# The last layer's K and V projections: in each group's step, or for all 16 groups at the fused stage's beginning

## The reference, cut to what matters

```python
qn = _layer_norm(x, ln1_g, ln1_b)               # x: output of layer 0
kn = vn = _layer_norm(ctx_1024, ln1_g, ln1_b)   # the context, the same for K and V
Q, K, V = qn @ wq + bq, kn @ wk + bk, vn @ wv + bv
attn = softmax(Q K^T / sqrt(8)) per head         # 16 heads of 8, not causal
x = x + (attn V) @ wo + bo
return x + gelu(_layer_norm(x) @ w1 + b1) @ w2 + b2
```

## Time and profile before

| | |
|---|---|
| median of 3 executions | 1389.48 us (1388.59 to 1390.74) |
| span of the profiled execution, first to last instruction | 1387.9 us |
| its own time as a whole | not given apart from the span; the median is 1.6 us above the span |
| mean granted clock of PE | 0.960 |
| busy over the span: PE, PEld, DVE, ACT, POOL | 89%, 75%, 68%, 71%, 65% |
| traffic | 113.96 MB, 82 GB/s in the mean |
| 900 to 1000 us (barrier, beginning of the fused stage): PE, DVE, ACT, POOL busy | 53, 55, 47, 66 of 100 us, PE clock 0.73 |
| 1000 to 1100 us (groups in full flow) | 89, 92, 88, 79 of 100 us, PE clock 1.00 |

### The profile page before, as it was taken

The page is one execution under the profiler, slowest core; times in us unless marked ns, Lnnn a source line. Parts: engine busy times, 40 slices in busy tenths (PEclk is TensorE's granted clock), DMA queues, the critical chain, the costliest instruction groups (busy, mean ns, idle before and its releaser), DMA issues. The chain is left out here.

```text
span 1387.9 us, 59975 instructions
## 1 busy us (share of the span) xinstructions
PE 1238.4 (89%) x23094; PEld 1036.4 (75%) x23094; DVE 944.3 (68%) x2136; ACT 980.7 (71%) x1956; POOL 897.7 (65%) x1432
## 2 busy tenths in 40 slices
PE   4999999989999998958999999925889998898997
PEld 2778888777788887937999999924677776675775
DVE  3788888877887886595555555525999999864331
ACT  1677787777888887346788776614888888875553
POOL 2577777777777665216999998758677777413431
PEclk9999999999999999579999999966999999999999
DMA  4233434332222320151322222322232333112221
GB/s 126 71 111 110 121 107 127 108 94 87 84 83 83 91 69 26 35 156 39 89 84 81 81 84 66 65 73 69 76 88 82 89 89 91 59 47 61 69 68 46
DMA packets 140285, 113.96 MB, mean 82 GB/s; under 512 B 17184, under 2 KB 113952, under 8 KB 140192
## 3 DMA queue, kind: packets, MB, share of 16 engines
q1 hardware_dynamic: 131744, 95.42, 23.5%
q0 software_dynamic: 8448, 17.32, 5.0%
HBM read 78.55 MB, written 34.08 MB: 81 GB/s over the span
## 5 line engine op out<-in xcount | busy, mean ns | idle before, releaser
L912 DVE TENSOR_REDUCE at_mx<-at_ps_s 128x16 f32<-128x1024 f32 x128 | 156.1, 1220 | 90.4 <-PE at_ps_s L599 46.3
L818 ACT ACTIVATE at_pt<-at_ps_t 128x1024 f32<-128x1024 f32 x128 | 130.6, 1020 | 54.7 <-PE at_ps_t L613 54.0
L811 ACT ACTIVATE at_pr<-at_dd 128x1024 f32<-128x1024 f32 x128 | 135.2, 1056 | 34.6 <-DVE at_dd L920 34.5
L2452 DVE COPY ex_wt<-experts 128x1156 f32 x133 | 102.8, 773 | 82.3 <-DVE ex_y L2458 74.0
L2410 ACT ACTIVATE ex_hg<-ex_ps_h,ex_wt 128x128 f32<-128x128 f32 x544 | 155.1, 375 | 1.2 <-PE ex_ps_y L2369 1.2
L2338 POOL DMA_INDIRECT ex_xg<-x,ex_ti x136 | 139.0, 1022 | 23.4 <-issue 21.8
L920 DVE TENSOR_TENSOR at_dd<-at_ps_s,at_mx 128x1024 f32<-128x1024 f32 x128 | 153.7, 1202 | 0.1
L2360 PE MATMUL ex_ps_h<-ex_xt,ex_wt 128*128 128x128 f32 x1088 | 147.1, 278 | 1.0 <-ACT ex_xt L2402 0.8
L1992 POOL DMA_INDIRECT l_yg<-rows,l_sl x128 | 126.1, 985 | 31.9 <-issue 29.5
L613 PE MATMUL at_ps_t<-ident,at_pr 128*128 128x128 f32 x1024 | 139.3, 279 | 6.1 <-issue 4.2
L2369 PE MATMUL ex_ps_y<-ex_wt,ex_hg 128*128 128x128 f32 x1088 | 143.7, 275 | 0.4 <-ACT ex_hg L2410 0.4
(11 more groups left out here) (262 smaller groups left out, 3154.5 us busy)
## 6 DMA issues: line engine op xcount, KB each, us to landing
rows<-ex_y SPq DMA_DIRECT2D x136, 64.0 KB
x<-at_ln_out SPq DMA_DIRECT2D x32, 256.0 KB, 3.2
at_kx<-in_xt SPq DMA_DIRECT2D x16, 256.0 KB, 2.8
at_qx<-in_xt SPq DMA_DIRECT2D x16, 256.0 KB, 2.8
at_vin<-in_xt SPq DMA_DIRECT2D x16, 256.0 KB, 2.9
at_xr<-in_x SPq DMA_DIRECT2D x16, 256.0 KB, 3.0
cx<-in_ctx SPq DMA_DIRECT2D x16, 256.0 KB, 3.2
x1t<-at_xt SPq DMA_DIRECT2D x16, 256.0 KB, 3.3
```

Source lines behind the costliest of these rows:

```text
L811: act.activation(pr[:, p], dd[:, p], ACT.Exp, scale=SCALE).then_inc(p_ready, 1)
L818: act.activation(pt[:, 2 * h + p], ps_t[:, :, :, :], ACT.Copy).then_inc(pt_ready, 1)
L912: dve.tensor_reduce(mx[:, p], ps_s[:, :, 4 * p:4 * p + 4, :], AX.X, ALU.max).then_inc(mx_ready, 1)
```

## The change

At the beginning of the fused stage PE projects K and V of all 16 groups, one after the other, out of the on-chip tile `x2t` (now called `zt` in this stage and kept alive to the end), in place of the 22 matmuls. K of group g goes into bank g % 2 of the score banks and ACT copies it back over `zt`; V goes into bank 2 + g % 2 and DVE copies it into one of 16 places in tiles that are not yet in use (`pt`, `dd`, `pr`), from where SP stores it to a memory tensor `ctxv`. These copies and stores are written into steps -3, -2 and -1 of the engines. In the steps proper `project_k` and `project_v` are gone: `mask_k` reads `zt`, and `copy_v` reads `vin`, which SP now loads from `ctxv`. The loads of `kx` and the stores of the transposed context in the two earlier stages are gone, with their waits. `hid` and `y` of the MLP now lie in `dd`.

```diff
 # sync engine, fused stage
-                    if a.shift(2).exists():
-                        load_k(a.shift(2))
+                def store_v(g):
+                    sp.wait_ge(vt_ready, g + 1)
+                    sp.dma_start(layer.kv_src[:, bass.ts(g, GT)], staged(g)).then_inc(v_out, 16)
+                    if a.unrolled and -3 <= a.g < 0:
+                        for g in ((0, 1, 2, 3, 4), (5, 6, 7, 8, 9, 10), (11, 12, 13, 14, 15))[a.g + 3]:
+                            store_v(g)
                     if a.shift(1).exists():
                         load_v(a.shift(1))            # the first waits for v_out, 16 * NG
 # tensor engine
-                spare = ps_s[:, 3].rearrange("p a b -> p (a b)")
-                pe.wait_ge(fmv_ready, 2)
-                for k in range(22):
-                    pe.matmul(spare[:, 0:P], c.ident[:, :], c.num[:, 0:P], start=True, stop=True)
+                for g in range(NG):
+                    project_k(g)                      # waits for kt_ready, g - 1
+                    project_v(g)                      # waits for vt_ready, g - 1
...
+                    else:                             # scores of the first half
+                        pe.wait_ge(kt_ready, NG)
+                        pe.wait_ge(vt_ready, NG)
...
-                        if a.shift(-1).exists():
-                            pe.wait_ge(vx_ready, g)
+                        if a.exists():
+                            pe.wait_ge(qb_ready, g + 1)
                         project_out(a.shift(-2))
...
-                    if a.shift(1).exists():
-                        pe.wait_ge(qb_ready, g + 2)
-                        project_k(a.shift(1))
...
-                    if a.exists():
-                        if a.shift(1).exists():
-                            pe.wait_ge(kb_ready, g + 2)
-                        else:
-                            pe.wait_ge(y_ready, g - 1)
-                        project_v(a)
 # scalar engine
+                def keep_k(g):
+                    act.wait_ge(early_k, g + 1)
+                    act.wait_ge(early_v, g + 1)
+                    act.activation(zt[:, bass.ts(g, GT)], bank[g % 2][:, :], ACT.Copy).then_inc(kt_ready, 1)
...
+                    if a.unrolled and -2 <= g < 0:    # first in the step
+                        for e in ((0, 1, 2, 3, 4, 5, 6, 7), (8, 9, 10, 11, 12, 13, 14, 15))[g + 2]:
+                            keep_k(e)
...
-                        ins = act.activation(kb[:, j, :], ps_g[:, :], ACT.Identity,
+                        ins = act.activation(kb[:, j, :], zt[:, bass.ts(a.place, GT)], ACT.Identity,
...
-                        src = ps_g[half, :].rearrange("p (w a m) -> p w a m", a=2, m=8)
+                        src = vin[half, :].rearrange("p (w a m) -> p w a m", a=2, m=8)
 # vector engine
+                def keep_v(g):
+                    dve.wait_ge(early_v, g + 1)
+                    dve.tensor_copy(staged(g), bank[2 + g % 2][:, :]).then_inc(vt_ready, 1)
...
+                    if a.unrolled and -3 <= g < -1:   # first in the step
+                        for e in ((0, 1, 2, 3, 4), (9, 10))[g + 3]:
+                            keep_v(e)
...
+                    if a.unrolled and -3 <= g < -1:   # after front_moments
+                        for e in ((5, 6, 7, 8), (11, 12, 13, 14, 15))[g + 3]:
+                            keep_v(e)
+                    if a.unrolled and g == -1:
+                        dve.wait_ge(v_out, 16 * NG)
                     if a.shift(1).exists():
                         maximum(g * 2 + 2, 0)
 # earlier stages
-                for g in range(NCT):
-                    sp.wait_ge(cxt_ready, g + 1)
-                    sp.dma_start(ct_out[:, bass.ts(g, GT)], layers[-1].out_tr[:, bass.ts(g, GT)]).then_inc(ct_stored, 16)
...
-                pool.wait_ge(r.ct_stored, 16 * NCT)
...
-                    if s == TU - 1 and turning:
-                        sp.dma_start(ct_out[:, bass.ts(q + NCT, GT)], xt_ctx[:, bass.ts(q + NCT, GT)]).then_inc(zc_stored, 16)
...
-                sp.wait_ge(zc_stored, 16 * (NG - NCT))
```

More of the change, by code:

```diff
@@ L1166, with __init__ @@
 class FinalStage:
-    def __init__(self, c, n, ps_s, ps_t, x_src, stored, scores_read, turned_read, w1_dram, b1_dram, w2_dram, b2, out_tok):
+    def __init__(self, c, n, ps_s, ps_t, x_src, stored, scores_read, turned_read, late, w1_dram, b1_dram, w2_dram, b2, out_tok):
         w1 = n.sb("w1", [P, FF])
@@ L1481, in fused_phase, with staged @@
         xb_ready, y_ready = n.sem("xb_ready"), n.sem("y_ready")
+        zt = layer.out_tr
+        bank = [ps_s[:, i].rearrange("p a b -> p (a b)") for i in range(4)]
+        def staged(g):
+            whole = (pt.rearrange("p h b r q -> p (h b r q)") if g < NG // 2 else
+                     dd.rearrange("p u r b s -> p (u r b s)") if g < 3 * NG // 4 else
+                     pr.rearrange("p u r b s -> p (u r b s)"))
+            return whole[:, bass.ts(g if g < NG // 2 else g % 4, GT)]
         def held(a):
@@ L1596, in widen, with project_k @@
                               stop=True).then_inc(r_ready, 1)
-                def project_k(a):
-                    pe.wait_ge(in_k, 16 * a.g + 16)
-                    pe.matmul(ps_g[:, :], layer.wk[:, :], kx[:, :], start=True, stop=True).then_inc(
-                        k_ready, 1)
+                def project_k(g):
+                    if g > 1:
+                        pe.wait_ge(kt_ready, g - 1)
+                    pe.matmul(bank[g % 2][:, :], layer.wk[:, :], zt[:, bass.ts(g, GT)], start=True, stop=True).then_inc(
+                        early_k, 1)
                 def project_q(a):
@@ L1613, in project_v @@
                         for j in range(2):
-                            mm = pe.matmul(ps_g[64 * j:64 * j + 64, t:t + SEQ], vin[:, t:t + SEQ],
-                                           w[:, :, j, :], start=True, stop=True)
-                    mm.then_inc(v_ready, 1)
+                            mm = pe.matmul(bank[2 + g % 2][64 * j:64 * j + 64, t:t + SEQ],
+                                           zt[:, GT * g + t:GT * g + t + SEQ], w[:, :, j, :], start=True, stop=True)
+                    mm.then_inc(early_v, 1)
                 def project_out(a):
@@ L1691, in _ @@
             def _(act):
+                def keep_k(g):
+                    act.wait_ge(early_k, g + 1)
+                    act.wait_ge(early_v, g + 1)
+                    act.activation(zt[:, bass.ts(g, GT)], bank[g % 2][:, :], ACT.Copy).then_inc(kt_ready, 1)
                 def mask_k(a):
-                    act.wait_ge(k_ready, a.g + 1)
+                    if a.unrolled and a.g == 0:
+                        act.wait_ge(kt_ready, NG)
                     if beyond(a.g, 0):
@@ L2504, in build @@
                 Layer(c, "sa", d["xt"], d["xt"], d["x"], x1, x1t, True, c.row["ln1_g"], c.row["ln1_b"], False, False),
[L2505 removed]
+                Layer(c, "ca", x1t, d["ctxt"], x1, x2, x2t, False, c.row["ln2_g"], c.row["ln2_b"], False, True, True)], d["ctx"], late)
             r.experts = m.sb("experts", [P, E, W])
@@ L2510, in build @@
             experts = ctx.enter_context(ExitStack())
-            done = expert_phase(nc, c, r, "ex_", x2, rows, x2t, ctxzt, done, experts)
+            done = expert_phase(nc, c, r, "ex_", x2, rows, x2t, done, experts)
             routing.close()
         fused_phase(nc, c, r, "l1_",
-                    Layer(c, "l1", None, ctxzt, x2, x4, None, False, None, None, True, False), x2, rows,
+                    Layer(c, "l1", None, ctxv, x2, x4, x2t, False, None, None, True, False), x2, rows,
                     (d["l1_w1"], d["l1_b1"], d["l1_w2"], c.row["l1_b2"], out), done)
```

50 lines of the change are left out of this document (22 added, 28 removed).

## The result

The changed kernel takes 1393.53 us (median of 20 runs, 1389.41 to 1399.14), the kernel before 1390.10 in the same comparison (20 runs, 1386.61 to 1397.55): ratio 1.0027, 95% interval 1.0015 to 1.0040. By the ratio it is 3.75 us slower, by the two medians 3.4. The forecast was 1392.4, on its bound between slower and same. A second comparison of the same two kernels, on another chip, gave 1.0010 (0.9998 to 1.0022), which by itself is not clear of no change. The loss is about 2 to 4 us, some 0.1 to 0.3%.

The account below looks back on a forecast made before the run. DVE was taken as the fullest engine, its two waits hanging on a chain without K and V projections. Start +4.4 and tail -1.5 gave +2.9 us on the 1387.9 span, 1390.8; with 1.6 added, 1392.4 us (range 1383 to 1397).

Parts of the forecast that it names:

- The loop: Steady steps of the fused stage: K and V leaving PE gain 0; bounds 0 and 16 us.
- The start: Fused stage's beginning: early projections and their copies move the first maximum from 960.67 to 965.05, +4.4 us.
- The gap at V13: Before V of group 13, PE idles 2.3 us awaiting DVE's copy; the clock then falls, adding 1.7 us.
- the 1.25 of the prediction: Front steps: DVE's five early V copies make POOL's first root, and every gather behind it, 1.25 us later.
- The shorter chain behind Q: Group 0, before the first scores: `mask_k` follows `mask_q` directly, making the chain 1.7 us shorter.
- The tail: Last steps, from step 13 on: PE's relief counts twice, -1.5 us in sum; bounds 0 and -3.
- the 0.6 that the prediction took for `copy_v`: Last steps: V no longer awaited and PE's turn before the multiplication earlier, 0.6 us less.
- The 0.9 before the exponential: Last steps: ACT's idle time before the exponential at 1232.18, scores late behind V; 0.9 us less (nothing to 1.2).
- V's stores: Wait for all V stores before the first maximum: 0 taken, bound +1 us.
- a rival of 0.10: Longer start, by stalls in unrolled code and slower gathers: +8 - 1.5, 1396 us; chance 0.10.
- The rival of relief: In the loop, PE's relief shrinks DVE's two waits: half of 16 us gives 1384.4 us; chance 0.20.
- The cheap start: Clock stays up through 2.3 us of idle PE, or falls late: +0.8 to +2.5, less 1.5, 1389.5 us; chance 0.26.

Follow-up runs that it names:

- relief: Changed kernel without any early K/V projections, copies or V stores, the 22 warm-up matmuls put back, outputs differing; 1387.82 us, ratio 0.9978 to the kernel before.
- fill: Copies placed as in interleave, plus 12 matmuls ahead of scores(0,0) and 18 ahead of scores(0,1); 1388.13 us, ratio 0.9992 to the kernel before.
- after: The changed kernel's first measurement and profile, its slowest execution of 20; median 1393.53 us, ratio 1.0027 to the kernel before.
- waits: Changed kernel plus 36 satisfied waits on PE's queue in the gap behind the last projection; ratio 1.0028 to the kernel before.
- after_again: The changed kernel unaltered, measured and profiled a second time; ratio 1.0010 to the kernel before.
- reorder: Changed kernel with V's copy of group 11 before the attention-input statistics and K's copy of group 15 behind group 0's scaling; ratio 1.0001 to the kernel before.
- before_fill: The kernel before plus 12 matmuls ahead of scores(0,0) and 18 ahead of scores(0,1); ratio 1.0024 to the unaltered kernel before.
- interleave: Changed kernel with V's copies of groups 4, 10, 11 between front-step pieces and K's of 14, 15 around scale_next(0); 1388.45 us, ratio 0.9993 to the kernel before.
- shim: Changed kernel plus 18 one-column matmuls (36 PE instructions) ahead of the stage's first matmul; ratio 1.0044 to the kernel before.

## Why the prediction was right, point by point

*The loop* (0): right. From the third on the distances agree within 0.04 us in all 14 profiles, relief's included; the second is 17.9 in all but fill, which has a stall there.

*The start* (+4.4 at the first maximum, to 52.8 from the stage's beginning): right in place and nearly in size. Three profiles with the changed start have 51.6, 52.5 and 51.5, two of before 48.4 and 47.6: +3.9. At the residual of group 0 it is +3.3 (92.9, 92.7, 92.4 against 90.0 and 88.6). Both are above the 0.8 to 1.4 us by which the two profiles of before differ. Of its terms:
- The gap at V13 was 1.63 us, not 2.3. The clock did not fall in it, so the 1.7 us of slow projections fell away. A pair took 2.14 us at full clock, not 2.05. V15 ended 38.7 and 38.6 us after the beginning in after and waits, not 40.4; in after_again it ended at 40.0, since there the clock rose 7.3 us after the beginning and not 4.7. (The prediction had PE stop 3.3 us before the clock fell near 983.2; by its own rows, 981.98 less 1.81, it was 3.0.)
- ACT's eight scalings behind the copy of K15 came as worked out, and the clock was at 0.50 for Q, 2.07 us. From `turn_z` to the end of the first scores the changed kernel took 8.9, 8.4 and 8.9 us and relief 7.4, so this clock cost 1.0 to 1.4, against 1.1 in the sum.
- POOL ended the roots of group 1 35.1 and 36.4 us after the beginning in the two profiles, 34.2 before: later by 0.9 and 2.2, around the 1.25 of the prediction. Behind PE's gate this didn't show; in reorder it did.
- The shorter chain behind Q is real: relief has its first maximum at 46.7, though the clock was low there too.

*The tail* (-1.5): the sign is right, the size and the place are not, and what stands beside it is larger. Both profiles of before have a stall in these steps, after_again has none, so their difference (52.5 against 54.2 and 54.7, -1.9) holds more than the term. before_fill runs exactly as before up to that stall and passes its place without one. These are ACT's rows of `copy_v` of the last group, first in before_fill, then in after_again:

```profile
1239.12 1.19 ACT L1728 ACTIVATE vx<-l_ps_g 64x512 f32<-64x512 f32 x2 [0.31 <-PE l_ps_g L1618]
...
1242.11 1.26 ACT L1729 ACTIVATE vx<-l_vin 64x512 f32<-64x512 f32 x2
```

From the residual of group 11 on they stand at 40.2 and 39.2 us, and before's at 41.0. So the change gave 1.0 us, and before's own stall made up the other 0.8; part of the 0.6 that the prediction took for `copy_v` was the wait behind that stall. The 0.9 before the exponential came as worked out, but DVE's `recip` behind it gave back a part: ACT's idle time ahead of `copy_o` grew from 1.67 to 1.90, and of the 1.4 us by which the exponential came sooner 0.6 are left there. And 0.35 of that 1.4 came in the step before, for which the prediction had none. With a stall or two in the changed kernel's tail the four distances are 56.3 and 56.6 (after and waits), +1.9 against before. The prediction had named an unexplained stall of 1.81 us as a risk of the start alone. The first distance adds 0.7 to 1.2 in the same way.

*V's stores*: right at the wait, where DVE shows no time for it, wrong at the gathers: slower gathers were left to a rival of 0.10, and in interleave those of group 1 landed 1.5 us later. No run separates the stores from the rest of the early work.

*Sum*: +3.3 at the residual of group 0, +1.0 in the first distance and -1.9 to +1.9 at the end give 2.4 to 6.2, against a measured 1.9 and 3.4 (the two differences of medians). That 2.9 lies between these two is in part luck: the start cost 1.1 less at the residual of group 0 than forecast, the tail's term was worth 1.0 and not 1.5, and stalls that stood in no term of the sum moved the time by as much either way.

The rival of relief is refuted. The cheap start is refuted as a whole, though its condition (a clock that stays up through the gap) came true; the clock still fell in the gap of 3.92 us ahead of `turn_z`. The clock did not fall in the loop: 1.00 over 1000 to 1230 us, with PE at 78.75 of 100 in the window above.

The Trainium skill (Runtime: NRT & Kernel Launch, section on instruction fetch mechanics) says that instructions are fetched in blocks of 256, at a cost that is mostly hidden. The traces agree with the blocks: the stalls stand at one place of a period of 256 instructions, each just behind a transfer on the instruction queue. They do not agree that it is hidden in this code, where PE runs through 256 small instructions in some 4 to 7 us: the stalls cost 0.4 to 2.7 us each, and more where the clock fell behind them. That stalls are what moved the ratio to 1.0024 in before_fill is likely but rests on one profile. What makes a transfer begin late in one execution and not in the next stays open.

## What to carry to other kernels

Work moved out of a loop into a stage's beginning isn't hidden because the engine that does it was idle: count who must drain it, and what stands behind the drain in those engines' orders. Here copies of 0.6 to 0.7 us on two other engines cost 3.3 us and, put between the pieces of the front steps, some 0.8 (90.2 against 90.0 and 88.6), which is within what two profiles of one kernel differ by.

Below 0.5% take at least two profiles of each kernel, and measure stages from a mark inside them. A change in the number of written-out instructions moves the places at which PE can stall for its next block, and such stalls are as large as the effect.

## What the runs showed of the hardware

- A matmul of one column is not smaller than one of 128: at clock 0.50 the 36 of 128x1 in shim began 0.21 us apart (7.81 us in all), and so did those of 128x128 in the kernel before (944.4 to 949.1). At clock 1.00 those of 128x128 began 0.11 us apart.
- PE's stalls with no releaser stand at the edges of blocks of 256 instructions and ended 1.20 to 1.57 us after the end of a transfer of 16384 bytes on the instruction queue (28 stalls of 0.42 to 2.65 us).
- An idle time of PE of 1.63 us (after) left the clock at 1.00; behind one of 3.92 us, and behind one of 1.51 us in the tail of waits, it was at 0.50.
- DVE's four operations with two inputs on chip took 2.70 to 2.76 us in the four kernels in which POOL's addition of 1.28 us fell into those of group 1, and 1.15 where it did not. Only one of the four is longer (in interleave 1.89 us and not 0.35), and it ends 0.15 us after the addition. The kernel before has the same at group 3, 2.92 us. The Trainium skill (SBUF — State Buffer, section on SBUF's two separate sides) has the two engines lock a shared port for a whole instruction, and whichever starts first gets it. The rows agree that DVE's operation waits for the whole addition; by their starts, though, DVE's had begun 0.46 us ahead of the addition, which the page's order doesn't explain.
